# Decoder attention: VectorE shifts two units of scores with one reduce and one add, from two neighbouring PSUM banks

## The chip, the cores and the metric

The kernel runs on one core of one Trainium2 chip. The metric is device time in microseconds, from the first to the last instruction of one execution. The engines are called PE (TensorE matmul), DVE (VectorE), ACT (ScalarE), POOL (GpSimd) and SP (SyncE, which only issues DMAs here). Each engine runs its own instructions strictly in the order in which the program lists them, and semaphores tie the engines together.

## The reference, cut to what matters

The program is a two-layer transformer block on 32 sequences of 128 tokens with 128 features. It has six stages, each followed by a layer norm: attention, windowed cross attention and routed experts in the first layer, and causal attention with rotary embedding, a gated recurrence and routed experts in the second. The change touches only the causal attention, which has 16 heads of 8 features:

```
qkv = x @ w_qkv
Q, K, V = split(qkv)                    # 16 heads of 8
Q, K = apply_rope(Q), apply_rope(K)
attn = einsum('bqhd,bkhd->bhqk', Q, K) * head_dim ** -0.5
attn = where(causal, attn, -1e9)
attn = softmax(attn, axis=-1)           # exp(attn - max) / sum
out = einsum('bhqk,bkhd->bqhd', attn, V).reshape(B, S, dim) @ w_proj + b_proj
x = layernorm(x + out)
```

## The kernel before

The kernel is one program with a function for each group of stages. `phase_decode` holds the decoder attention. It works sequence by sequence (32 of them, index `b`) and cuts the 16 heads of a sequence into four *units* of four heads, so there are 128 units. One unit's scores are 128 queries by 4 x 128 keys in fp32, which fill one PSUM bank exactly. The tensor `quad` (`d_bank_scores`) is four banks next to each other, one for each unit of a sequence.

Time is cut into *ticks*, one for each unit, and every engine has one loop over the same ticks. `due(tick, offset)` says whether a step of some sequence falls on this tick; each such step falls on every fourth tick. Four ticks, in which the four units u0 to u3 of one sequence pass, are called a *frame* here. The order within an engine is thus written out by hand, and nothing reorders it.

What one frame holds on each engine, in its order, with the lines of the kernel before:

- PE: at tick 3 of a frame it writes the causal mask into banks 2 and 3 (L1644), then adds the next sequence's scores to all four banks (L1651), and signals `scores_done`. After that come, for units u2 and u3 of the frame and u0 and u1 of the next, the turning of the probabilities (`turn`, L1660) and the product with the values (`weigh`, L1672). In between stand: the turn back of an output (L1747, `mix_back`), the projections of the coming sequence into the bank `vec_bank` (L1704, `qk_done`) and of its values (L1709), two turns (L1717 and L1724), the output projection (L1729), and at tick 2 the mask for banks 0 and 1.
- DVE: for each unit the negated row maximum (L1802, `d_neg_max`) and the add that shifts the scores (L1806, into the ring `sc`, signal `shifted`). After u0 it scales a mixed output out of `vec_bank` (L1809 reciprocal and L1812 multiply, signal `mix_scaled`), after u1 it takes the rotary products from `vec_bank` (L1819, `d_halves`), and after u3 come eleven small instructions of two layer norms (L1828 to L1903).
- ACT: for each unit the exponential (L1765, waits for `shifted`), and the copy of the turned probabilities (L1783). Between them stand copies of other banks: the mixed output (L1762), the turned mix (L1772, `d_mixT`, signal `mixT_ready`), the values (L1768) and others.

`vec_bank` and `act_bank` are each shared by several steps in turn, so waits order them: PE may write the projections (L1704) only once DVE has scaled the output that lay in `vec_bank` (L1812), and may turn x4 into `act_bank` (L1724) only once ACT has taken `mixT` from it (L1772). In code:

```
if (n := due(tick, -8)) is not None:          # PE, tick 0 of a frame
    pe.wait_ge(x4T_ready, n + 1)
    if n >= 4:
        pe.wait_ge(mix_scaled, n - 3)
...
if (n := due(tick, -10)) is not None:         # PE, tick 2 of a frame
    pe.wait_ge(x4_ready, n + 1)
    if n >= 5:
        pe.wait_ge(mixT_ready, n - 4)
```

Of the kernel before, what the change touches and what calls it, by code (L numbers as in the profile page):

```python
# [14 lines left out]
P = 128  # L15
# [88 lines left out]
def bcast(ap, n):  # L104

    return ap.unsqueeze(2).to_broadcast([ap.shape[0], ap.shape[1], n])
# [1422 lines left out]
def phase_decode(nc, c, d, keep, scr, xT_all, experts1, recur):  # L1529
# [4 lines left out]
    with Phase(nc) as ctx:  # L1534
# [3 lines left out]
        def tiles(name, shape, n=2):  # L1538
            return ring(nc, ctx, "d_" + name, shape, n)

        def bank(name):
# [8 lines left out]
                                    tiles("x4_bo", [P, P], 7))  # L1550
        halves, qk, k_place, va = (tiles("halves", [P, G, P]), tiles("q_k_rotated", [P, 2, P]), tiles("k_by_place", [P, G, P]),
                                   tiles("values", [P, HEADS, VC], 4))
        nmax, sc, pr, pt = (tiles("neg_max", [P, G], 4), tiles("scores", [P, G, P], 4), tiles("probs", [P, G, P], 3),
                            tiles("probs_t", [P, G * P]))
        ot, rs, mix, mixT = tiles("mix_t", [P, G * P]), tiles("rsum", [P, HEADS]), tiles("mix", [P, P]), tiles("mixT", [P, P])
        sub5, x5 = tiles("sub5", [P, P]), tiles("x5", [P, P])
# [83 lines left out]
        @block.tensor  # L1640
        def _(pe):
            def mask(b, g):

                nc.tensor.matmul(quad[:, g, :], lhsT=c["ident_bf"][:], rhs=repeat(c["causal_bf"][:], G), start=True, stop=False)  # L1644

            def scores(b):

                pe.wait_ge(k_ready, b + 1)
                for g in range(G):
                    rows = slice(32 * g, 32 * g + 32)  # L1650
                    last = nc.tensor.matmul(quad[:, g, :], lhsT=qk[b % 2][rows, 0, :],  # L1651
                                            rhs=k_place[b % 2][rows, :, :].rearrange("p j u -> p (j u)"), start=False, stop=True)
                last.then_inc(scores_done, 1)

            def turn(u):
                pe.wait_ge(probs_ready, u + 1)
                if u:
                    pe.wait_ge(probs_t_ready, u)
                for j in range(G):
                    last = nc.tensor.transpose(turned_bank[:, j * P:(j + 1) * P], pr[u % 3][:, j, :], c["ident"][:])  # L1660
                last.then_inc(probs_turned, 1)

            def weigh(u):

                b, g = divmod(u, G)
                pe.wait_ge(probs_t_ready, u + 1)
                if g == 0:
                    pe.wait_ge(v_ready, b + 1)
                    if b:
                        pe.wait_ge(mix_copied, b)  # L1670
                for j in range(G):
                    last = nc.tensor.matmul(mix_bank[32 * j:32 * j + VC, g * P:(g + 1) * P], lhsT=va[b % 4][:, G * g + j, :],  # L1672
                                            rhs=pt[u % 2][:, j * P:(j + 1) * P], start=True, stop=True)
                last.then_inc(mixed, 1)

            pe.wait_ge(buffers_set, 2)
            for g in range(G):
                mask(0, g)
            for tick in TICKS:
                b, g = divmod(tick, G)  # L1680
                if g == G - 1 and 0 <= b + 1 < BATCH:
                    if b >= 0:
                        for bank in (2, 3):
                            pe.wait_ge(shifted, b * G + bank + 1)
                            mask(b + 1, bank)
                    scores(b + 1)
                if g == 1 and 2 <= tick < UNITS_ALL + 2:
                    weigh(tick - 2)
                if 1 <= tick <= UNITS_ALL:
                    turn(tick - 1)  # L1690
                if g != 1 and 2 <= tick < UNITS_ALL + 2:
                    weigh(tick - 2)
                if g == 2 and 0 <= b < BATCH - 1:
                    for bank in (0, 1):
                        pe.wait_ge(shifted, b * G + bank + 1)
                        mask(b + 1, bank)
                if (n := due(tick, -8)) is not None:
                    pe.wait_ge(x4T_ready, n + 1)
                    if n >= 4:
                        pe.wait_ge(mix_scaled, n - 3)  # L1700
                    elif n:
                        pe.wait_ge(halves_ready, n)
                    for k, name in enumerate(("l_wq", "l_wk", "l_wqp", "l_wkp")):
                        last = nc.tensor.matmul(vec_bank[:, k * P:(k + 1) * P], lhsT=c[name][:], rhs=x4T[n % 2][:],  # L1704
                                                start=True, stop=True)
                    last.then_inc(qk_done, 1)
                    if n >= 7:
                        pe.wait_ge(x5T_ready, n - 6)
                    nc.tensor.matmul(act_bank[:, 0:P], lhsT=x4T[n % 2][:], rhs=c["l_wv"][:], start=True, stop=True)\  # L1709
                        .then_inc(v_done, 1)  # L1710
                if (n := due(tick, 9)) is not None:
                    pe.wait_ge(mix_scaled, n + 1)
                    if n + 4 < BATCH:
                        pe.wait_ge(v_ready, n + 5)
                    else:
                        pe.wait_ge(x5T_ready, n - 2)
                    nc.tensor.transpose(act_bank[:, 0:P], mix[n % 2][:], c["ident"][:]).then_inc(mix_turned, 1)  # L1717
                if (n := due(tick, -10)) is not None:
# [3 lines that stand above are left out]
                    elif n:  # L1722
                        pe.wait_ge(v_ready, n)
                    nc.tensor.transpose(act_bank[:, 0:P], x4[n % 2][:], c["ident"][:]).then_inc(x4_transposed, 1)  # L1724
                if (n := due(tick, 10)) is not None:
                    pe.wait_ge(mixT_ready, n + 1)
                    if n + 4 < BATCH:
                        pe.wait_ge(halves_ready, n + 5)
                    nc.tensor.matmul(vec_bank[:, 0:P], lhsT=mixT[n % 2][:], rhs=c["l_wo"][:], start=True, stop=True)\  # L1729
                        .then_inc(attn_done, 1)  # L1730
                if (n := due(tick, 19)) is not None:
                    pe.wait_ge(x5_ready, n + 1)
                    if n + 7 < BATCH:
                        pe.wait_ge(x4T_ready, n + 8)
                    elif n + 2 < BATCH:
                        pe.wait_ge(mixT_ready, n + 3)
                    else:
                        pe.wait_ge(x5T_ready, n)
                    nc.tensor.transpose(act_bank[:, 0:P], x5[n % 2][:], c["ident"][:]).then_inc(x5_turned, 1)
                if (n := due(tick, 7)) is not None:  # L1740
                    pe.wait_ge(mix_copied, n + 1)
                    if n:
                        pe.wait_ge(joined5, n)
                    else:
                        pe.wait_ge(halves_ready, 4)
                    for k in range(G):
                        last = nc.tensor.transpose(vec_bank[:, k * P:(k + 1) * P], ot[n % 2][:, k * P:(k + 1) * P], c["ident"][:])  # L1747
                    last.then_inc(mix_back, 1)
                if -21 <= tick < -4:
                    stream(nc, c, turned_bank[:, 0:2 * P])  # L1750
                if tick == UNITS_ALL + 4:
                    pe.wait_ge(probs_t_ready, UNITS_ALL)
                if UNITS_ALL + 4 <= tick:
                    stream(nc, c, turned_bank[:, 0:P])

        @block.scalar
        def _(act):
            act.wait_ge(buffers_set, 2)
            for tick in TICKS:
# [1 line left out]
                    act.wait_ge(mixed, G * b + G)  # L1761
                    nc.scalar.activation(ot[b % 2][:], mix_bank[:], ACT.Copy).then_inc(mix_copied, 1)  # L1762
                if 0 <= tick < UNITS_ALL:
                    act.wait_ge(shifted, tick + 1)
                    nc.scalar.activation(pr[tick % 3][:], sc[tick % 4][:], ACT.Exp).then_inc(probs_ready, 1)  # L1765
                if (b := due(tick, -7)) is not None:
                    act.wait_ge(v_done, b + 1)
                    nc.scalar.activation(va[b % 4][:, :, 0:DH], act_bank[:, 0:P].rearrange("p (h d) -> p h d", d=DH), ACT.Copy)\  # L1768
# [18 lines left out]
        def _(dve):  # L1787
# [7 lines left out]
            chain = Chain(dve, links, 0, 0)  # L1795

            for tick in TICKS:
                if 0 <= tick < UNITS_ALL:
                    b, g = divmod(tick, G)
                    dve.wait_ge(scores_done, b + 1)  # L1800
                    bank = quad[:, g, :].rearrange("p (j u) -> p j u", j=G)
                    nc.vector.tensor_reduce(nmax[tick % 4][:], bank, AX.X, ALU.max, negate=True).then_inc(max_ready, 1)  # L1802
                    dve.wait_ge(max_ready, tick + 1)
                    if tick >= 4:
                        dve.wait_ge(probs_ready, tick - 3)
                    nc.vector.tensor_tensor(sc[tick % 4][:], bank, bcast(nmax[tick % 4][:], P), ALU.add).then_inc(shifted, 1)  # L1806
                if (b := due(tick, 8)) is not None:
                    dve.wait_ge(mix_back, b + 1)
                    nc.vector.reciprocal(rs[b % 2][:], vec_bank[:].rearrange("p (h c) -> p h c", c=VC)[:, :, DH])\  # L1809
# [742 lines left out]
```

## Time and profile before

| | us |
|---|---|
| three runs | 1351.29, 1352.99, 1353.49 (median 1352.99) |
| the profiled execution | 1351.8 |
| its span in the trace | 1350.0 |
| busy in the span: PE / DVE / ACT / POOL | 1180.8 / 1043.2 / 855.9 / 555.8 |
| decoder attention, first to last start of L1802 | 810.9 to 1093.2 |
| of that, L1806 x128 / L1802 x128 busy | 88.5 / 87.4 |

The span is from the first instruction to the last in the trace. Busy is the sum of the instructions' own durations on an engine; a group that is pipelined can look busy while it does not run at its peak. The decoder attention takes some 285 of the 1350 us.

### The profile page before, as it was taken

Reading aid. Unit: us, or ns where it says so; the run is one execution under the profiler, and the core shown is the slowest. Engines: PE = TensorE matmul, PEld = TensorE weight load, DVE = VectorE, ACT = ScalarE, POOL = GpSimd, SP = SyncE. Lnnn points to the kernel's source line nnn. Section 1 sums busy time; section 2 is a strip of 40 time slices with the busy share of each in tenths; the row PEclk is TensorE's granted clock in tenths of the full one; section 3 lists DMA queues with packets and bytes.
Section 4 is the critical chain, followed back from the end, with each engine's and each line's share of the span. In section 5 each row is a group of like instructions: output and inputs, shape, how many; then the busy total and the mean of one; then the engine's idle time right before and its main releaser. Section 6 shows DMA issues by size and latency. Waiting matters only on the chain. (4 is left out here: it accounts for less than half of the span.)

```text
span 1350.0 us, 31833 instructions
## 1 busy us (share of the span) xinstructions
PE 1180.8 (87%) x10209; PEld 817.6 (61%) x10209; DVE 1043.2 (77%) x3188; ACT 855.9 (63%) x2442; POOL 555.8 (41%) x831
## 2 busy tenths in 40 slices
PE   3789999999999999887399978999999979999796
PEld 2556665666666666654266655555555557767796
DVE  4578889888888888876688858999999965665465
ACT  2678888888788878854166625666666654453464
POOL 1233334434353535351400046555555312556387
PEclk9999999999999999997599988999999989999898
DMA  6200000000010100000222222103000000000673
GB/s 225 95 15 15 17 15 23 24 19 29 17 33 15 31 11 25 10 20 11 65 81 82 83 57 90 38 24 97 25 21 19 2 3 1 17 17 25 180 211 93
DMA packets 71490, 63.54 MB, mean 47 GB/s; under 512 B 10510, under 2 KB 61586, under 8 KB 70688
## 3 DMA queue, kind: packets, MB, share of 16 engines
q1 hardware_dynamic: 62768, 45.27, 11.4%
q0 software_dynamic: 6400, 12.63, 3.0%
q10 hardware_dynamic: 2160, 3.60, 0.8%
q8 instruction: 87, 1.43, 0.4%
q14 instruction: 75, 0.61, 0.1%
HBM read 45.10 MB, written 16.88 MB: 46 GB/s over the span
## 5 line engine op out<-in xcount | busy, mean ns | idle before, releaser
L783 PE MATMUL e_bank_turned<-c_matrices,e_probs 128*128 128x128 f32 x1024 | 164.6, 285 | 19.0 <-ACT e_probs_t L1008 9.2
L709 POOL TENSOR_TENSOR e_rstd<-e_var_eps,c_minus_half 128x1 f32<-128x1 f32 x128 | 71.2, 570 | 234.6 <-DVE e_var_eps L1049 233.7
L1008 ACT ACTIVATE e_probs_t<-e_bank_turned 128x512 f32<-128x512 f32 x256 | 154.8, 605 | 14.5 <-PE e_bank_turned L783 12.9
L1136 DVE TENSOR_REDUCE e_neg_max<-e_bank_scores 128x4 f32<-128x512 f32 x160 | 109.7, 685 | 49.2 <-PE e_bank_scores L827 48.4
L783 PEld LDWEIGHTS e_bank_turned<-c_matrices,e_probs 128*128 128x128 f32 x1024 | 115.8, 144 | 43.8 <-issue 22.6
L793 PE MATMUL e_bank_mix<-e_probs_t,e_values 128*32 128x128 f32 x2048 | 111.6, 291 | 16.0 <-ACT e_probs_t L1008 15.8
L971 ACT ACTIVATE e_probs<-e_scores,e_neg_max 128x128 f32<-128x128 f32 x384 | 123.4, 411 | 1.1 <-DVE e_neg_max L1172 1.1
L1783 ACT ACTIVATE d_probs_t<-d_bank_turned 128x512 f32<-128x512 f32 x128 | 77.2, 603 | 66.1 <-PE d_bank_turned L1660 66.1
L966 ACT ACTIVATE e_probs<-e_scores 128x512 f32<-128x512 f32 x128 | 81.7, 638 | 43.0 <-DVE e_scores L1169 41.3
L712 POOL TENSOR_TENSOR e_k_by_place<-e_q_k_k,c_matrices 128x512 f32<-128x512 f32 x64 | 66.7, 1042 | 100.4 <-DVE e_q_k_k L1180 100.4
L1765 ACT ACTIVATE d_probs<-d_scores 128x512 f32<-128x512 f32 x128 | 81.0, 633 | 41.0 <-DVE d_scores L1806 39.3
L1660 PE MATMUL d_bank_turned<-c_matrices,d_probs 128*128 128x128 f32 x512 | 82.3, 284 | 24.7 <-ACT d_probs_t L1783 23.6
L1660 PEld LDWEIGHTS d_bank_turned<-c_matrices,d_probs 128*128 128x128 f32 x512 | 55.6, 142 | 61.4 <-issue 56.6
L1806 DVE TENSOR_TENSOR d_scores<-d_bank_scores,d_neg_max 128x512 f32<-128x512 f32 x128 | 88.5, 692 | 4.4
L1802 DVE TENSOR_REDUCE d_neg_max<-d_bank_scores 128x4 f32<-128x512 f32 x128 | 87.4, 683 | 5.7 <-PE d_bank_scores L1651 5.5
L1169 DVE TENSOR_TENSOR e_scores<-e_bank_scores,e_neg_max 128x512 f32<-128x512 f32 x128 | 88.3, 690 | 3.4
L1601 POOL DMA_INDIRECT d_first<-scratch_expert_out,keep_out_rows x32 | 32.2, 1005 | 137.8 <-POOLq L85 132.1
L793 PEld LDWEIGHTS e_bank_mix<-e_probs_t,e_values 128*32 128x32 f32 x2048 | 40.8, 109 | 63.0 <-issue 33.8
L1342 PE MATMUL m_wide<-up,m_rowsT 128*128 x144 | 75.8, 609 | 0.4 <-ACT m_rowsT L1407 0.2
L720 POOL DMA_INDIRECT scratch_sorted<-e_x,e_row_u x64 | 64.3, 1005 | 26.5 <-issue 15.8
L2120 ACT ACTIVATE n_states<-n_bank_drive 128x32 f32<-128x32 f32 x128 | 25.3, 198 | 65.1 <-PE n_bank_drive L2046 63.0
L1138 DVE TENSOR_TENSOR e_scores<-e_bank_scores,c_bias 128x512 f32<-128x512 f32 x96 | 65.7, 684 | 0.0
(324 smaller groups left out, 3232.7 us busy)
## 6 DMA issues: line engine op xcount, KB each, us to landing
streamed<-in_s_up SPq DMA_DIRECT2D x36, 258.0 KB, 2.9
sorted_rows<-scratch_sorted SPq DMA_DIRECT2D x72, 64.0 KB, 1.8
scratch_expert_out<-m_y SPq DMA_DIRECT2D x72, 64.0 KB
sorted_rows<-scratch_sorted SPq DMA_DIRECT2D x40, 65.0 KB, 2.3
e_xT_ctxT<-in_xT SPq DMA_DIRECT2D x32, 64.0 KB
e_xT_ctxT<-in_ctxT SPq DMA_DIRECT2D x32, 64.0 KB
e_x_in<-in_x SPq DMA_DIRECT2D x32, 64.0 KB, 1.8
up<-in_m_wgv SPq DMA_DIRECT2D x1, 2048.0 KB
```

Of the source, the lines that this page charges most:

```text
L783: last = nc.tensor.transpose(turned_bank[:, j * P:(j + 1) * P], pr[k % 3][:, j, :], c["ident"][:])
L793: last = nc.tensor.matmul(mix_bank[32 * j:32 * j + VC, g * P:(g + 1) * P], lhsT=va[att][n % 3][:, G * g + j, :], rhs=pt[k % 2][:, j * P:(j ...
L966: nc.scalar.activation(pr[k % 3][:], sc[k % 4][:], ACT.Exp).then_inc(probs_ready, 1)
L971: last = nc.scalar.activation(pr[k % 3][:, j, :], src[:, j, :], ACT.Exp, bias=nmax[k % 4][:, j:j + 1], scale=1.0)
L1008: nc.scalar.activation(pt[k % 2][:], turned_bank[:], ACT.Copy).then_inc(probs_t_ready, 1)
L1136: nc.vector.tensor_reduce(nmax[k % 4][:], bank, AX.X, ALU.max, negate=True).then_inc(max_ready, 1)
L1169: nc.vector.tensor_tensor(sc[k % 4][:], bank, bcast(nmax[k % 4][:], P), ALU.add).then_inc(bank_read, 1)
L1660: last = nc.tensor.transpose(turned_bank[:, j * P:(j + 1) * P], pr[u % 3][:, j, :], c["ident"][:])
L1765: nc.scalar.activation(pr[tick % 3][:], sc[tick % 4][:], ACT.Exp).then_inc(probs_ready, 1)
L1783: nc.scalar.activation(pt[(tick - 1) % 2][:], turned_bank[:], ACT.Copy).then_inc(probs_t_ready, 1)
L1802: nc.vector.tensor_reduce(nmax[tick % 4][:], bank, AX.X, ALU.max, negate=True).then_inc(max_ready, 1)
L1806: nc.vector.tensor_tensor(sc[tick % 4][:], bank, bcast(nmax[tick % 4][:], P), ALU.add).then_inc(shifted, 1)
```

## The change

DVE now works at ticks 0 and 2 of a frame only, each time on two banks: one reduce over 128 x 8 x 128 scores and one add of the same size. The ring `sc` has two buffers of two units in place of four of one, and `shifted` counts pairs. ACT's exponentials stay one for each unit, and each waits for its pair. PE waits for a pair before it writes the masks of two banks. Nothing else is touched; lines below the edit move by one.

```diff
-        nmax, sc, pr, pt = (tiles("neg_max", [P, G], 4), tiles("scores", [P, G, P], 4), tiles("probs", [P, G, P], 3),
+        nmax, sc, pr, pt = (tiles("neg_max", [P, 2 * G], 4), tiles("scores", [P, 2 * G, P]), tiles("probs", [P, G, P], 3),
...
                     if b >= 0:
+                        pe.wait_ge(shifted, 2 * b + 2)
                         for bank in (2, 3):
-                            pe.wait_ge(shifted, b * G + bank + 1)
                             mask(b + 1, bank)
...
                 if g == 2 and 0 <= b < BATCH - 1:
+                    pe.wait_ge(shifted, 2 * b + 1)
                     for bank in (0, 1):
-                        pe.wait_ge(shifted, b * G + bank + 1)
                         mask(b + 1, bank)
...
                 if 0 <= tick < UNITS_ALL:
-                    act.wait_ge(shifted, tick + 1)
-                    nc.scalar.activation(pr[tick % 3][:], sc[tick % 4][:], ACT.Exp).then_inc(probs_ready, 1)
+                    pair, half = divmod(tick, 2)
+                    act.wait_ge(shifted, pair + 1)
+                    nc.scalar.activation(pr[tick % 3][:], sc[pair % 2][:, half * G:(half + 1) * G, :], ACT.Exp).then_inc(probs_ready, 1)
...
-                if 0 <= tick < UNITS_ALL:
-                    b, g = divmod(tick, G)
+                if 0 <= tick < UNITS_ALL and tick % 2 == 0:
+                    (b, g), pair = divmod(tick, G), tick // 2
                     dve.wait_ge(scores_done, b + 1)
-                    bank = quad[:, g, :].rearrange("p (j u) -> p j u", j=G)
-                    nc.vector.tensor_reduce(nmax[tick % 4][:], bank, AX.X, ALU.max, negate=True).then_inc(max_ready, 1)
-                    dve.wait_ge(max_ready, tick + 1)
-                    if tick >= 4:
-                        dve.wait_ge(probs_ready, tick - 3)
-                    nc.vector.tensor_tensor(sc[tick % 4][:], bank, bcast(nmax[tick % 4][:], P), ALU.add).then_inc(shifted, 1)
+                    banks_of_pair = quad[:, g:g + 2, :].rearrange("p g (j u) -> p (g j) u", j=G)
+                    nc.vector.tensor_reduce(nmax[pair % 4][:], banks_of_pair, AX.X, ALU.max, negate=True).then_inc(max_ready, 1)
+                    dve.wait_ge(max_ready, pair + 1)
+                    if pair >= 2:
+                        dve.wait_ge(probs_ready, tick - 2)
+                    nc.vector.tensor_tensor(sc[pair % 2][:], banks_of_pair, bcast(nmax[pair % 4][:], P), ALU.add).then_inc(shifted, 1)
```

The first place is DVE's order in one frame. Before, from the first reduce of a frame to the first instruction of its layer norms (the names are tiles, written `out<-in`):

```order
L1802 TENSOR_REDUCE d_neg_max<-d_bank_scores 128x4
L1806 TENSOR_TENSOR d_scores<-d_bank_scores,d_neg_max 128x512
L1809 RECIPROCAL d_rsum<-d_bank_vec 128x16
L1812 TENSOR_TENSOR d_mix<-d_bank_vec,d_rsum 128x128
L1802 TENSOR_REDUCE d_neg_max<-d_bank_scores 128x4
L1806 TENSOR_TENSOR d_scores<-d_bank_scores,d_neg_max 128x512
L1819 TENSOR_TENSOR d_halves<-d_bank_vec,c_rope 128x512
L1802 TENSOR_REDUCE d_neg_max<-d_bank_scores 128x4
L1806 TENSOR_TENSOR d_scores<-d_bank_scores,d_neg_max 128x512
L1802 TENSOR_REDUCE d_neg_max<-d_bank_scores 128x4
L1806 TENSOR_TENSOR d_scores<-d_bank_scores,d_neg_max 128x512
```

And the same stretch of DVE's row with the change:

```order
L1803 TENSOR_REDUCE d_neg_max<-d_bank_scores 128x8
L1807 TENSOR_TENSOR d_scores<-d_bank_scores,d_neg_max 128x1024
L1810 RECIPROCAL d_rsum<-d_bank_vec 128x16
L1813 TENSOR_TENSOR d_mix<-d_bank_vec,d_rsum 128x128
L1820 TENSOR_TENSOR d_halves<-d_bank_vec,c_rope 128x512
L1803 TENSOR_REDUCE d_neg_max<-d_bank_scores 128x8
L1807 TENSOR_TENSOR d_scores<-d_bank_scores,d_neg_max 128x1024
```

The work of u1 has moved ahead of the scaling (L1809, L1812), and nothing stands between the scaling and the rotary products (L1819) any more.

The second place is ACT's order from tick 2 of a frame to tick 3, the same before and with the change but for the numbers of the lines; here with the change, where both exponentials wait for the pair u2, u3:

```order
L1762 ACTIVATE d_mix_t<-d_bank_mix 128x512
L1766 ACTIVATE d_probs<-d_scores 128x512
L1773 ACTIVATE d_mixT<-d_bank_act 128x128
L1784 ACTIVATE d_probs_t<-d_bank_turned 128x512
L1766 ACTIVATE d_probs<-d_scores 128x512
```

The copy of `mixT` and the copy of the turned probabilities of u1 stand behind the exponential of u2, as before.

## Rows read from the trace of the kernel before

**Rows 1.** Busy us (x count) of PE, PEld, DVE, ACT, POOL; granted clock; DMA share, GB/s.

```profile
950.00:1000.00 50.00, 45.63 (x437) 28.08 (x435) 47.33 (x124) 32.66 (x74) 28.67 (x38) 1.00 0.08 24
```

**Rows 2.** Timeline of DVE: the first reduce of frames 2 and 30.

```profile
829.38 0.69 DVE L1802 TENSOR_REDUCE d_neg_max<-d_bank_scores 128x4 f32<-128x512 f32 x1 [0.26 <-PE d_bank_scores L1651]
...
1080.35 0.69 DVE L1802 TENSOR_REDUCE d_neg_max<-d_bank_scores 128x4 f32<-128x512 f32 x1 [0.51 <-PE d_bank_scores L1651]
```

**Rows 3.** Timeline of one frame: start, us, engine, instruction, [idle before <-releaser].

```profile
953.76 0.59 PE L1644 MATMUL d_bank_scores<-c_causal_bf,c_ident_bf 128*128 128x512 bf16 x2
...
955.50 0.69 DVE L1802 TENSOR_REDUCE d_neg_max<-d_bank_scores 128x4 f32<-128x512 f32 x1 [0.19 <-PE d_bank_scores L1651]
956.22 0.69 DVE L1806 TENSOR_TENSOR d_scores<-d_bank_scores,d_neg_max 128x512 f32<-128x512 f32 x1
...
957.11 0.26 DVE L1809 RECIPROCAL d_rsum<-d_bank_vec 128x16 f32<-128x16 f32 x1 [0.19 <-PE d_bank_vec L1747]
957.40 0.29 DVE L1812 TENSOR_TENSOR d_mix<-d_bank_vec,d_rsum 128x128 f32<-128x128 f32 x1
...
957.61 0.68 DVE L1802 TENSOR_REDUCE d_neg_max<-d_bank_scores 128x4 f32<-128x512 f32 x1
957.83 1.13 PE L1704 MATMUL d_bank_vec<-d_x4T,c_matrices 128*128 128x128 f32 x8
958.32 0.69 DVE L1806 TENSOR_TENSOR d_scores<-d_bank_scores,d_neg_max 128x512 f32<-128x512 f32 x1
959.05 0.63 ACT L1765 ACTIVATE d_probs<-d_scores 128x512 f32<-128x512 f32 x1 [0.77 <-DVE d_scores L1806]
959.17 0.69 DVE L1819 TENSOR_TENSOR d_halves<-d_bank_vec,c_rope 128x512 f32<-128x512 f32 x1 [0.16 <-PE d_bank_vec L1704]
...
959.78 0.68 DVE L1802 TENSOR_REDUCE d_neg_max<-d_bank_scores 128x4 f32<-128x512 f32 x1
...
960.91 0.63 PE L1660 MATMUL d_bank_turned<-c_matrices,d_probs 128*128 128x128 f32 x4 [0.62 <-ACT d_probs_t L1783]
961.23 0.63 ACT L1765 ACTIVATE d_probs<-d_scores 128x512 f32<-128x512 f32 x1
...
962.27 0.27 PE L1724 MATMUL d_bank_act<-c_matrices,d_x 128*128 128x128 f32 x1
...
962.60 0.59 PE L1644 MATMUL d_bank_scores<-c_causal_bf,c_ident_bf 128*128 128x512 bf16 x2
```

**Rows 4.** Timeline at the decoder's end: PE waits for the scaled mix.

```profile
1100.98 0.29 DVE L1812 TENSOR_TENSOR d_mix<-d_bank_vec,d_rsum 128x128 f32<-128x128 f32 x1
...
1101.33 0.48 PE L1717 MATMUL d_bank_act<-c_matrices,d_mix 128*128 128x128 f32 x1 [0.38 <-DVE d_mix L1812]
```

**Rows 5.** Timeline of frame 1: DVE waits for the projections.

```profile
823.07 1.16 PE L1704 MATMUL d_bank_vec<-d_x4T,c_matrices 128*128 128x128 f32 x8
...
824.27 0.69 DVE L1819 TENSOR_TENSOR d_halves<-d_bank_vec,c_rope 128x512 f32<-128x512 f32 x1 [0.68 <-PE d_bank_vec L1704]
```

**Rows 6.** Timeline of frame 14: u2's exponential, the copy behind it, and PE.

```profile
943.34 0.63 ACT L1765 ACTIVATE d_probs<-d_scores 128x512 f32<-128x512 f32 x1 [0.63 <-DVE d_scores L1806]
943.87 0.26 ACT L1772 ACTIVATE d_mixT<-d_bank_act 128x128 f32<-128x128 f32 x1
...
944.28 0.30 PE L1724 MATMUL d_bank_act<-c_matrices,d_x 128*128 128x128 f32 x1 [0.40 <-ACT d_mixT L1772]
```

**Rows 7.** The same columns in frame 0 and behind the last frame.

```profile
817.50:820.00 2.50, 2.50 (x12) 0.80 (x10) 1.59 (x5) 0.28 (x1) 2.40 (x5) 0.50 0.58 131
...
1097.50:1100.00 2.50, 1.28 (x12) 0.66 (x13) 0.38 (x2) 1.27 (x4) 0.00 (x0) 1.00 0.00 0
1100.00:1102.50 2.50, 2.10 (x10) 1.62 (x11) 1.44 (x6) 1.85 (x4) 0.55 (x1) 0.63 0.00 0
```

**Rows 8.** Timeline of frame 0: masks to the next reduce.

```profile
817.70 1.06 PE L1644 MATMUL d_bank_scores<-c_causal_bf,c_ident_bf 128*128 128x512 bf16 x2
...
820.85 0.69 DVE L1802 TENSOR_REDUCE d_neg_max<-d_bank_scores 128x4 f32<-128x512 f32 x1 [1.69 <-PE d_bank_scores L1651]
```

## The prediction

> **What bounds the kernel now.** I read the busy time by stretch first. In 950 to 1000 us, steady decoder work, DVE is busy 47.33 of 50 us and PE 45.63 at the full clock [rows 1]. Two engines that are both over 90% busy invite the conclusion that work taken off DVE shortens the stage. Busy time cannot decide that, since two in-order engines that wait for each other in turn can both look full. So I read the timeline next, frame by frame. Frames 2 to 29, 28 of them, take 1080.35 - 829.38 = 250.97 us, or 8.96 us each [rows 2].
>
> One frame [rows 3] is followed from the mask of banks 2 and 3 at 953.76 to the same mask at 962.60, 8.84 us later. The scores let DVE's first reduce start 1.74 us after the mask; DVE had waited 0.19 for it. The reciprocal at 957.11 had waited 0.19 for PE's turn back, not for DVE's own work, so u0's reduce and add had that much slack. After the scaling at 957.40, PE writes the projections into the same bank at 957.83, and DVE takes the rotary products at 959.17, having waited 0.16 us. Between the scaling and the rotary products DVE did the whole of u1 (957.61 and 958.32). That work covered the way to PE and back. Further on, PE turns u1's probabilities at 960.91 after a wait of 0.62 for ACT, and reaches the turn of x4 at 962.27 and the next mask at 962.60. ACT began u2's exponential at 961.23 without an idle gap.
>
> The frame is therefore a ring of short hops through PE, DVE and ACT, with slack of only tenths. I price the change on that ring.
>
> **What the change does to DVE's own time.** An instruction over 512 columns lets the next one start 0.61 us later (959.17 to 959.78), one over 128 columns 0.21 (957.40 to 957.61): 0.40 us for 384 columns, so 512 more columns cost 0.53 [rows 3]. Reduce to add, where the add must wait for the reduce's result, takes 0.72 (955.50 to 956.22) and should become 0.72 + 0.53 = 1.25. Add to the next instruction should become 0.61 + 0.53 = 1.14. A pair takes 2.39 where two units took 2 x (0.72 + 0.61) = 2.66: 0.27 less, and 0.27 x 64 = 17 us over all pairs. No row shows a DVE instruction that reads two banks. The dearest case is no saving at all, 1.44 and 1.22. For the other end I allow 0.1 us off a whole frame, from the spread of equal hops in the rows. I take the extrapolation, since a doubled instruction is nearest to the row of 512 columns plus its slope.
>
> The page "Advanced Engine Details and Errata" of the Trainium skill, section "The Read-Write Bubble", advises large tiles of 512 or 1024 elements, and one instruction over several PSUM banks, to pay a gap between instructions less often. The slope above bears the advice out as far as DVE's own time goes; by that alone the sum would be the third rival below.
>
> **Ring, first half: the scaling comes late.** The scaling now stands behind the work of both units. From the mask: 1.74 to the reduce, 1.25 to the add, 1.14 to the reciprocal, 0.29 to the multiply (957.11 to 957.40) [rows 3]. From the multiply to PE I have 0.35 where PE waited (1100.98 to 1101.33) [rows 4] and 0.43 in the frame, where PE may have had work of its own; I take 0.40. That makes 4.82 us from the mask to the projections, against 957.83 - 953.76 = 4.07. PE's earlier work, which took the 4.07, no longer sets it. Queued behind the waiting projections are the values' projection, the product for u3 and the turn of the next u0; all come 0.75 later.
>
> **Ring, second half: the cover is gone.** DVE's next instruction is the one that waits for those projections. They took 1.20 us to reach DVE where it really waited, 0.68 us of it (823.07 to 824.27) [rows 5], and 1.34 in the frame of [rows 3]; I take 1.20. Then 0.61 to the reduce of u2 and u3, and 1.25 to their add. ACT's exponential began 0.73 after an add's start (958.32 to 959.05, a real wait) [rows 3] and now begins 0.73 + 0.53 = 1.26 after it. So u2's exponential starts 1.20 + 0.61 + 1.25 + 1.26 = 4.32 us after the projections; before it was 961.23 - 957.83 = 3.40.
>
> What is queued behind that exponential decides. The copy of `mixT` follows 0.53 later (943.34 to 943.87), and PE may turn x4 0.41 after that, a row in which PE did wait 0.40 for it [rows 6]; 0.33 more brings the next mask (962.27 to 962.60) [rows 3]. In the frame before, 961.23 + 0.53 + 0.41 = 962.17 was 0.10 ahead of the turn at 962.27: hidden, but barely. Now the sum is 4.32 + 0.53 + 0.41 + 0.33 = 5.59 us from the projections to the next mask, against 962.60 - 957.83 = 4.77.
>
> **The rest of the edit costs nothing.** The wait for masks 2 and 3 is over long before: the add of u2 and u3 ends about 1.25 us after its start, at the time ACT's exponential begins, and the mask stands 1.27 behind that (0.53 + 0.41 + 0.33). The masks of banks 0 and 1 wait for a pair that is done before PE's projections start. The smaller ring of buffers waits for exponentials of the pair two before, a frame earlier. DVE's layer norms now begin 1.26 + 1.27 - 1.14 = 1.39 us before the mask; in [rows 3] the first reduce waited for the scores though DVE came from the same norms, so the first hop stays at 1.74. POOL's preparation of the keys starts with the rotary products, and the mask ahead of the scores now comes 5.59 - 1.20 = 4.39 us after these, where it was 962.60 - 959.17 = 3.43.
>
> **The sum.** 4.82 + 5.59 = 10.41 us a frame in place of 8.96: 1.45 x 28 = 40.6 us. At both ends the first exponential of a pair comes 1.25 + 1.26 - (0.72 + 0.73) = 1.06 later. I put 2 us for the two ends. The profiled execution took 1351.8 us (span 1350.0), so 1351.8 + 42.6 = 1394 us. The median of the runs, 1352.99, is 1.2 above that execution, less than any case here differs by.
>
> If a pair saves nothing, each frame adds 2 x 0.19 for the reduces, 0.08 before the reciprocal and 0.20 before the exponential, 0.66 x 28 = 18 us: 1412. If the hops are 0.1 shorter, it is 1391.
>
> **Rivals.**
>
> *Only the first half counts.* If the copy of `mixT` is not what PE waits for, the second half stays as it is and the frame grows by 0.75: 21 us and 2 at the ends, 1375. For it: in the frame of [rows 3] PE did not wait at that turn. Against it: the slack was 0.10, and the exponential comes 0.92 later.
>
> *PE's clock falls.* PE would idle some 2.2 us of each 10.4: 0.75 ahead of the projections, 0.62 ahead of u1's turn as now, 0.82 ahead of the turn of x4. Behind the last frame a stretch with PE busy 1.28 of 2.5 us was followed by one at a mean granted clock of 0.63, a fall to 1.2 GHz from 2.4 [rows 7]. In the new frame the last two of these gaps, 1.44 us, fall within some 3 us, not far from that row's 1.22 idle in 2.5. At 1.2 GHz (0.50 in the stretch of frame 0 [rows 7]) the hop from mask to reduce took 3.15 us (817.70 to 820.85) [rows 8] and not 1.74. A third of the frames at that price add 9 x 1.41 = 13: 1407. All of them would give 1434.
>
> *DVE is the bound, and the time falls.* Then the 17 us saved are gained: 1335. For it: 47.33 of 50 us [rows 1]. It is also what the advice on large tiles quoted above from the Trainium skill comes to. It holds only if the hops from scaling to rotary products, 0.40 + 1.20 less the 0.21 that DVE spends there anyway, 1.39 us, came to less than the 0.54 that a frame saves. Against it: [rows 5] shows DVE waiting when nothing covers that way.
>
> *The change doesn't do what it says.* If PE's own work sets the frame whatever DVE does, nothing moves: 1352. Against it: the reciprocal now comes 1.25 + 1.14 = 2.39 us after the first reduce, where it was 957.11 - 955.50 = 1.61 [rows 3], and 0.19 us of slack do not cover 0.78.
>
> **How the numbers follow.** Chances: the forecast 0.62, the falling clock 0.17, only the first half 0.10, DVE as the bound 0.06, no change 0.05. A measurement of this kernel tells about 0.2% from nothing, some 3 us. So faster 0.06, same 0.05, slower 0.89. The range takes in the first rival at its low end and, at the high end, the pair without savings and a clock that falls in more than a third of the frames: 1372 to 1418.
>
> **What would show it.** Right: frames of about 10.4 us; L1803 and L1807 near 1.2 us each; L1820 waiting about a microsecond for PE's L1704 in each frame; ACT's L1766 waiting for DVE before u2, and PE waiting for ACT's L1773 before it turns x4; DVE's share down to some 75%. Wrong: L1820 without a wait, frames under 9 us, or a granted clock below 1.00 in the middle of the decoder, which would put the time above the forecast.

## The result, and the profile after

The changed kernel is slower: a median of 1400.57 us in 4 runs (1395.99 to 1403.88) against 1353.24 for the kernel before on the same chip (1351.29 to 1353.72), a ratio of 1.035 with a 95% interval of 1.0326 to 1.0374. Its profiled execution took 1403.88 us, its span is 1402.0.

Busy time by stretch, kernel after, columns as in [rows 1]:

```profile
950.00:1000.00 50.00, 40.42 (x379) 24.51 (x378) 37.94 (x89) 27.79 (x63) 24.34 (x33) 1.00 0.28 71
```

DVE is down from 47.33 us of 50 to 37.94 and PE from 45.63 to 40.42, at the full granted clock. Every engine has more free time, which fits engines that wait for each other; the timeline below shows the waits. The DMA share is higher because the weights of the next stage begin to load at 951.16 us here and at 927.21 before; the frames are as long outside that burst. Next the timeline of DVE, kernel after, first reduces of frames 2 and 30, as in [rows 2]:

```profile
837.69 1.22 DVE L1803 TENSOR_REDUCE d_neg_max<-d_bank_scores 128x8 f32<-128x1024 f32 x1 [0.69 <-PE d_bank_scores L1651]
...
1131.33 1.23 DVE L1803 TENSOR_REDUCE d_neg_max<-d_bank_scores 128x8 f32<-128x1024 f32 x1 [0.51 <-PE d_bank_scores L1651]
```

The 28 frames take 293.64 us, 10.49 each, where they took 8.96. One of them, timeline of PE, DVE and ACT in the kernel after, as in [rows 3]:

```profile
961.88 0.59 PE L1644 MATMUL d_bank_scores<-c_causal_bf,c_ident_bf 128*128 128x512 bf16 x2
...
963.62 1.23 DVE L1803 TENSOR_REDUCE d_neg_max<-d_bank_scores 128x8 f32<-128x1024 f32 x1 [0.44 <-PE d_bank_scores L1651]
...
964.87 1.23 DVE L1807 TENSOR_TENSOR d_scores<-d_bank_scores,d_neg_max 128x1024 f32<-128x1024 f32 x1
...
966.01 0.25 DVE L1810 RECIPROCAL d_rsum<-d_bank_vec 128x16 f32<-128x16 f32 x1
...
966.30 0.29 DVE L1813 TENSOR_TENSOR d_mix<-d_bank_vec,d_rsum 128x128 f32<-128x128 f32 x1
...
966.74 1.13 PE L1704 MATMUL d_bank_vec<-d_x4T,c_matrices 128*128 128x128 f32 x8 [0.76 <-DVE d_mix L1813]
...
967.90 0.69 DVE L1820 TENSOR_TENSOR d_halves<-d_bank_vec,c_rope 128x512 f32<-128x512 f32 x1 [1.31 <-PE d_bank_vec L1704]
...
968.51 1.21 DVE L1803 TENSOR_REDUCE d_neg_max<-d_bank_scores 128x8 f32<-128x1024 f32 x1
...
969.76 1.23 DVE L1807 TENSOR_TENSOR d_scores<-d_bank_scores,d_neg_max 128x1024 f32<-128x1024 f32 x1
...
971.02 0.63 ACT L1766 ACTIVATE d_probs<-d_scores 128x512 f32<-128x512 f32 x1 [0.86 <-DVE d_scores L1807]
971.55 0.26 ACT L1773 ACTIVATE d_mixT<-d_bank_act 128x128 f32<-128x128 f32 x1
...
971.96 0.30 PE L1724 MATMUL d_bank_act<-c_matrices,d_x 128*128 128x128 f32 x1 [0.63 <-ACT d_mixT L1773]
972.09 0.45 PE L1729 MATMUL d_bank_vec<-c_matrices,d_mixT 128*128 128x128 f32 x2
...
972.38 0.59 PE L1644 MATMUL d_bank_scores<-c_causal_bf,c_ident_bf 128*128 128x512 bf16 x2
```

Read it as a relay. PE stands 0.76 us until DVE has scaled the mix behind the adds of both units; DVE then stands 1.31 us, its dearest idle spot in the decoder, until the projections are there; PE stands 0.63 until ACT has copied `mixT` behind u2's exponential. From the mask of banks 2 and 3 to the projections it is 4.86 us, from the projections to the next such mask 5.64. Over the whole run, groups of DVE's instructions in the kernel after (count | busy us, mean ns | idle ahead):

```profile
L1807 DVE TENSOR_TENSOR d_scores<-d_bank_scores,d_neg_max 128x1024 f32<-128x1024 f32 x64 | 78.4, 1224 | 2.2
L1803 DVE TENSOR_REDUCE d_neg_max<-d_bank_scores 128x8 f32<-128x1024 f32 x64 | 78.0, 1219 | 16.8 <-PE d_bank_scores L1651 16.8
L1820 DVE TENSOR_TENSOR d_halves<-d_bank_vec,c_rope 128x512 f32<-128x512 f32 x32 | 22.1, 690 | 37.7 <-PE d_bank_vec L1704 37.7
```

DVE did become cheaper: 78.4 + 78.0 us of add and reduce, where the two groups took 88.5 and 87.4 before. What it saved went into waiting, 37.7 us of it in one place.

The two spans differ by 52.0 us: 42.7 in the 28 frames, 0.7 ahead of frame 2, 1.0 behind the start of frame 30, and 7.6 before the decoder's first reduce (818.44 against 810.9), in stages that the edit does not touch. That last part is not the change's: in the ten kernels below, which are all alike ahead of the decoder, this reduce starts between 809.88 and 818.74 us.

### The profile page after: what moved, and what is told of

It is laid out like the page before. It is cut to its first block and busy times, and to the rows that moved or that the text cites. A ratio compares the mean times of both kernels' runs of the same rounds, so it can differ in the third digit from the quotient of the medians.

```text
span 1402.0 us, 31643 instructions
## 1 busy us (share of the span) xinstructions
PE 1192.8 (85%) x10209; PEld 819.5 (58%) x10209; DVE 1029.0 (73%) x3060; ACT 854.8 (61%) x2442; POOL 553.7 (39%) x831
## 5 line engine op out<-in xcount | busy, mean ns | idle before, releaser
L1803 DVE TENSOR_REDUCE d_neg_max<-d_bank_scores 128x8 f32<-128x1024 f32 x64 | 78.0, 1219 | 16.8 <-PE d_bank_scores L1651 16.8
L1807 DVE TENSOR_TENSOR d_scores<-d_bank_scores,d_neg_max 128x1024 f32<-128x1024 f32 x64 | 78.4, 1224 | 2.2
L1172 DVE TENSOR_REDUCE e_neg_max<-e_scores 128x4 f32<-128x512 f32 x96 | 64.8, 675 | 0.3
```

Source lines behind the costliest of these rows:

```text
L1803: nc.vector.tensor_reduce(nmax[pair % 4][:], banks_of_pair, AX.X, ALU.max, negate=True).then_inc(max_ready, 1)
L1807: nc.vector.tensor_tensor(sc[pair % 2][:], banks_of_pair, bcast(nmax[pair % 4][:], P), ALU.add).then_inc(shifted, 1)
```

## The experiments

All kernels are in one table; "frame" is the mean of the 28 frames of [rows 2], the two halves of the ring are means over frames 6 to 25, and "rest" is the span from the decoder's first reduce to the end. Ratios are to the kernel before in the same batch (its medians 1352.57, 1350.56 and 1350.35).

| kernel | median us | ratio (95%) | frame | mask to proj. | proj. to mask | rest |
|---|---|---|---|---|---|---|
| before | 1353.24 | | 8.96 | 4.07 | 4.95 | 539.1 |
| after | 1400.57 | 1.035 (1.0326-1.0374) | 10.49 | 4.85 | 5.64 | 583.6 |
| early pair only | 1376.70 | 1.018 (1.0161-1.02) | 9.67 | 4.91 | 4.76 | 559.7 |
| late pair only | 1395.09 | 1.0306 (1.0285-1.0327) | 10.35 | 4.16 | 6.33 | 580.0 |
| both, copy first | 1375.41 | 1.0171 (1.0153-1.0189) | 9.62 | 4.85 | 4.77 | 558.7 |
| both, scaling between | 1396.37 | 1.0327 (1.03-1.0353) | 10.16 | 4.10 | 6.16 | 579.6 |
| late pair, gather moved | 1376.68 | 1.0206 (1.0177-1.0234) | 9.78 | 4.09 | 5.72 | 561.4 |
| late pair, copy first | 1352.18 | 1.0009 (0.9991-1.0026) | 8.87 | 4.07 | 4.82 | 536.2 |
| both, all moved | 1354.17 | 1.0025 (1.001-1.0041) | 8.88 | 4.07 | 4.83 | 538.8 |
| before, copy first | 1350.62 | 1.0 (0.9984-1.0016) | 8.90 | 4.07 | 4.86 | 535.5 |
| before, gather moved | 1354.80 | 1.0019 (0.9999-1.0039) | 8.91 | 4.17 | 4.77 | 535.4 |
| late, copy first, gather moved | 1353.67 | 1.002 (0.9999-1.004) | 8.89 | 4.15 | 4.76 | 537.0 |

The theory is the ring: a pair costs what stands behind it in DVE's and ACT's queues. One rival is that the pair itself, the wait for two banks, sets the price; another is PE's clock.

**Each pair alone.** From the kernel before; the early pair reads `g != 1` and `g == 0` in place of `g != 3` and `g == 2`.

```diff
-                if 0 <= tick < UNITS_ALL:
-                    b, g = divmod(tick, G)
+                b, g = divmod(tick, G)
+                if 0 <= tick < UNITS_ALL and g != 3:
+                    units, pair, low = 2 if g == 2 else 1, tick // 2, g % 2 * G
```

Early pair (u0 and u1):

> Only u0 and u1 are taken as a pair; u2 and u3 stay single, as before. Theory: mask to projections stays at 4.85 us as in the changed kernel; u2's exponential then starts 1.17 + 0.61 + 0.72 + 0.73 = 3.23 us after the projections, before ACT is free for it at 3.40, so the second half is that of before, 4.77 to 4.98; frames of 9.62 to 9.83, 1372 to 1378. Rival A (all of the loss comes from the late scaling): frames stay at 10.5, 1396 to 1400. If only the late exponential counted: 8.96, 1353.

1376.70 us, as expected. The first half took 4.91 us, 0.84 more than before; the second took 4.76, which is what the shortest frames before took (their mean is 4.95). A frame costs 0.71 us more, though u2's exponential is not late: the late scaling has that price by itself.

Late pair (u2 and u3):

> Only u2 and u3 are taken as a pair; u0 and u1 stay single, with the scaling between them, as before. Theory (two hops of the ring, each with its own price): mask to projections goes back to 4.07 us, projections to the next mask stays at the 5.64 of the changed kernel, since u2's exponential still waits for the pair; frames of 9.71 us, 0.75 x 28 = 21 us over before: about 1374. Rival A (all of the loss comes from the late scaling): frames of 8.96, 1353. Rival B (a DVE instruction that reads two banks is itself what slows its neighbours): the hops around the pair lengthen and not the waits, about 1375 as well, but with DVE's add over 1.3 us or PE's and ACT's instructions on those banks longer.

1395.09 us: a miss by 21. The first half was as before, but the hop from the projections to the rotary products took 1.74 to 1.84 us in 20 frames instead of 1.17. (In two frames the granted clock fell as well; they took 11.98 and 11.87 us.) Timeline of POOL, PE and DVE in this kernel, one such frame and the one frame between them that was spared:

```profile
957.90 1.13 PE L1704 MATMUL d_bank_vec<-d_x4T,c_matrices 128*128 128x128 f32 x8
958.19 0.96 POOL L1601 DMA_INDIRECT d_second<-scratch_expert_out,keep_out_rows  x1 [0.30 <-issue]
...
959.70 0.69 DVE L1823 TENSOR_TENSOR d_halves<-d_bank_vec,c_rope 128x512 f32<-128x512 f32 x1 [0.63 <-PE d_bank_vec L1704]
...
968.80 0.95 POOL L1601 DMA_INDIRECT d_second<-scratch_expert_out,keep_out_rows  x1 [0.30 <-issue]
...
970.30 1.13 PE L1704 MATMUL d_bank_vec<-d_x4T,c_matrices 128*128 128x128 f32 x8 [0.38 <-issue]
...
971.46 0.69 DVE L1823 TENSOR_TENSOR d_halves<-d_bank_vec,c_rope 128x512 f32<-128x512 f32 x1
```

Where POOL's second gather of a coming sequence's rows starts 0.29 us behind the projections, the rotary products start 1.80 behind them; where it starts 1.50 ahead, 1.16. PE's own time is 1.13 in both. The spared frame is one of the two in which the clock fell (0.59 in 965 to 968): its projections came 5.91 us behind the mask, not 4.07, and the gather had not waited for them. So a third thing seemed to be in this ring, and the next kernel moves only that.

**Late pair, gather moved.** In each frame the two gathers now stand right behind POOL's preparation of the keys, ahead of its three small layer-norm steps and no longer behind them. The expectations call this later; for a given sequence it is one tick earlier.

```diff
-                if (b := due(tick, -25)) is not None:
+                if (b := 0 if tick == FIRST else due(tick, -26)) is not None:
                     gather(b)
```

> The kernel with only the late pair (u2 and u3), and POOL's gather of the next frame issued after its placing of the mask's row, one step later in the tick than before. Theory that the frames of the late-pair kernel were long because DVE's rotary products wait while POOL issues the second gather 0.3 us behind the projections: the hop from the projections to the halves goes back from 1.74 to 1.84 us to 1.17, frames take about 9.68 us, and the run about 1,374 to 1,378 us, some 20 us less than the late pair alone. Rival, that the late pair itself makes that hop long (the gather only happens to lie there): frames stay at 10.4 us and the run at 1,392 to 1,396. In between: the gather meets another DVE instruction of the ring instead (the layer norms ahead of the reduce), and the loss shows there as a longer hop from the projections' first row to the mask.

1376.68 us, 18 less. Timeline of POOL, PE and DVE in this kernel:

```profile
954.83 0.96 POOL L1601 DMA_INDIRECT d_second<-scratch_expert_out,keep_out_rows  x1 [0.30 <-issue]
...
959.34 1.13 PE L1704 MATMUL d_bank_vec<-d_x4T,c_matrices 128*128 128x128 f32 x8
...
960.51 0.69 DVE L1823 TENSOR_TENSOR d_halves<-d_bank_vec,c_rope 128x512 f32<-128x512 f32 x1
```

The hop was 1.17 (1.16 to 1.18) in all of the 28 frames. They took 9.78 us, 0.1 more than expected. The late pair with the gather out of the way costs 0.82 us a frame, of which 0.77 lie in the second half, as the theory has it.

**Both pairs, copy of `mixT` first.** From the changed kernel, on ACT:

```diff
+                if (b := due(tick, 10)) is not None:
+                    act.wait_ge(mix_turned, b + 1)
+                    nc.scalar.activation(mixT[b % 2][:], act_bank[:, 0:P], ACT.Copy).then_inc(mixT_ready, 1)
                 if 0 <= tick < UNITS_ALL:
...
-                if (b := due(tick, 10)) is not None:
-                    act.wait_ge(mix_turned, b + 1)
-                    nc.scalar.activation(mixT[b % 2][:], act_bank[:, 0:P], ACT.Copy).then_inc(mixT_ready, 1)
```

> Both pairs, as in the changed kernel; ACT copies mixT ahead of u2's exponential instead of behind it, so that nothing of PE's stands behind that wait. Theory: mask to projections 4.85, projections to the next mask back to 4.77 to 4.98: frames of 9.62 to 9.83, about 1375, some 20 us less than the changed kernel. Rival A (all of the loss comes from the late scaling): no gain, frames stay at 10.5. Rival B (the two-bank instructions themselves): no gain either.

1375.41 us. Timeline of ACT and PE in this kernel:

```profile
950.89 0.28 ACT L1765 ACTIVATE d_mixT<-d_bank_act 128x128 f32<-128x128 f32 x1
...
951.86 0.63 ACT L1769 ACTIVATE d_probs<-d_scores 128x512 f32<-128x512 f32 x1 [0.69 <-DVE d_scores L1807]
952.02 0.27 PE L1724 MATMUL d_bank_act<-c_matrices,d_x 128*128 128x128 f32 x1
952.13 0.39 PE L1729 MATMUL d_bank_vec<-c_matrices,d_mixT 128*128 128x128 f32 x2
...
952.35 0.59 PE L1644 MATMUL d_bank_scores<-c_causal_bf,c_ident_bf 128*128 128x512 bf16 x2
```

The copy is done before u2's exponential begins, PE no longer waits at L1724, and the second half is back at 4.77. One copy of 128 columns, placed behind an exponential that it does not need, was 0.87 us a frame.

**Both pairs, scaling between reduce and add.** From the changed kernel; `scale` is the reciprocal and the multiply.

```diff
                     nc.vector.tensor_reduce(nmax[pair % 4][:], banks_of_pair, AX.X, ALU.max, negate=True).then_inc(max_ready, 1)
+                    if (n := due(tick, 8)) is not None:
+                        scale(n)
                     dve.wait_ge(max_ready, pair + 1)
```

> Both pairs; DVE scales the mixed output between the reduce and the add of the first pair instead of behind the add, so that the add covers the way to PE and back. Theory: mask to projections back to 4.07. But u0's exponential now comes later, 3.84 + 1.26 = 5.10 us after the mask, and ACT's copy of the turned u3 of the frame before stands behind it (5.8), for which PE's product waits: that would carry u0's turn to about 6.9 and the next mask to 10.0 to 10.3. So the frame hardly gains, 10.0 to 10.3: 1384 to 1391. Without this last wait the frame would be 9.72, 1376. Rival A (all of the loss comes from the late scaling): 8.96, 1353.

1396.37 us, only 4 less than the changed kernel and 5 above the expected range. The first half fell to 4.07 in ordinary frames, as expected, but the next step in line became the wait. Timeline of ACT and PE in this kernel:

```profile
899.59 0.37 ACT L1781 ACTIVATE xT_all<-d_bank_act 128x128 f32<-128x128 f32 x1
...
900.01 0.49 PE L1709 MATMUL d_bank_act<-c_matrices,d_x4T 128*128 128x128 f32 x2 [0.85 <-ACT xT_all L1781]
```

PE's value projection waits 0.85 us for another copy that ACT keeps behind an exponential, that of u0, which the pair made late. The expectation had named the copy of the turned u3, which stands next behind the same exponential. Ordinary frames take 9.96 us, just below the 10.0 to 10.3 expected. In four of the 28 the granted clock falls as well; busy time by stretch, columns as in [rows 1]:

```profile
878.00:881.00 3.00, 1.79 (x17) 1.26 (x18) 2.97 (x5) 2.58 (x8) 1.77 (x2) 0.96 0.08 22
881.00:884.00 3.00, 3.00 (x18) 1.73 (x18) 0.85 (x4) 2.17 (x6) 0.00 (x0) 0.50 0.33 113
```

0.50 is 1.2 GHz; PE had been busy 1.79 of 3 us ahead of the fall. Such frames take 11.5 us, which lifts the mean to 10.16 and the run by some 6 us.

**Both pairs, all of these moved.** The scaling between, and ACT's copies of `mixT`, of `xT_all` and of the turned u3 ahead of the exponentials.

> Both pairs, as in the changed kernel, with all the steps that the ring was found to wait for moved ahead: the scaling between the first pair's reduce and subtraction, ACT's copy of mixT ahead of the exponential of u2, its copies of the value input and of the turned u3 ahead of the exponential of u0. Theory that pairing costs only by what stands behind the pair in the queues: frames of 8.84 to 9.1 us, 1,349 to 1,356 us, about as the kernel before. If the wait for both banks itself (PE's second bank, not the queue) sets the price: frames of 9.6 us or more and over 1,371 us. If clock falls come, as with the scaling moved alone, single frames show 1 us or more on top and a mean of 9.2 to 9.3.

1354.17 us, frames of 8.88. The pairs are all still there, and the loss is gone but for 0.25%. Busy time by stretch:

```profile
950.00:1000.00 50.00, 47.13 (x447) 29.15 (x446) 44.88 (x98) 33.32 (x74) 29.86 (x39) 1.00 0.09 23
```

DVE is 2.45 us lighter than in [rows 1] and PE 1.50 fuller. From the decoder's first reduce to the end the profiled execution takes 538.8 us, before 539.1. The 28 frames gained 2.2 us, and the ends gave most of it back: the granted clock fell at the very end (0.70 in 1086 to 1089), and the last frame took 10.24 us, before 8.13. One profile of each does not settle where the 0.25% lies. What holds the frame at 8.9 is probably PE, busy 94% here; no run took work off PE, so that is argued only.

**Late pair, copy first.**

> The late pair alone, with ACT's copy of mixT put ahead of the exponential of u2, so that the projections no longer wait for that exponential. Without a meeting with POOL's gather the first half of the ring takes 4.07 us and the second, now free of the copy behind the exponential, about 4.8 to 5.0: frames of 8.84 to 9.05 us, 1,350 to 1,356 us, no different from the kernel before. If the gather still meets the rotary products (0.6 us more in most frames): 9.4 to 9.6 us and 1,366 to 1,371 us. If pairing as such costs more than the order of ACT's copy, frames stay above 10 us and the run above 1,385.

1352.18 us, no difference from before. Once the copy stands ahead of it, the pair of u2 and u3 costs nothing that shows (at most 0.26% by the interval).

**Control: the kernel before, copy first.**

> Control: the kernel before, with only ACT's copy of mixT put ahead of the exponential of u2. In the kernel before the exponential of u2 ends 1.7 us or so behind its bank and the copy stands behind it, but there the add of u2 and the exponential come after the mask's subtraction of another tick. If the copy waits for it there too, frames shrink from 8.96 to 8.84 us and the run to 1,349 to 1,350 us; if not, 1,352 to 1,353, no difference. Either way the move alone gives no 25 us, so that what it gives back in the changed kernel is the price of the pair and not a gain that was there to be had anyway.

1350.62 us, ratio 1.0, with frames of 8.90 us, between the 8.84 and the 8.96 of the two cases. What the move returns in the changed kernel is the pair's price, not a gain that lay there anyway.

**The gather in the kernel before, and with the late pair.**

> The kernel before, with only POOL's gathers issued after the placing of the mask's row (as in the late pair with the later gather). Theory that a gather that starts some 0.5 to 0.84 us behind the projections holds DVE's rotary products: the hop from the projections to the halves goes from a mean of 1.33 us to 1.17 in every frame, ordinary frames from 8.97 to 8.83, and the run 3 to 5 us down, to about 1,346 to 1,348. If the gather in its new place holds another DVE instruction of the ring (as the layer norm and the late subtraction were held by 0.05 to 0.1 us in the late pair with the later gather), the gain is 1 us or none. If the gather has nothing to do with it, the hop keeps its 1.33 and the run its 1,351 to 1,353.

> The late pair with ACT's copy of mixT first and the gathers later. By the same theory the hop from the projections to the halves goes from a mean of 1.36 us to 1.17. The second half of the ring is then 0.2 us shorter, unless the first half and the other rings of the frame stand at 8.83 us already, which is the shortest frame of the run without the later gather: frames of 8.83 us throughout, 1,349 to 1,351 us against 1,352 for the one with the gather in its old place. A pair that beat the kernel before by 0.2% or more (below 1,348 us) would show that the pair itself is of use once its wait is covered; 1,349 or more, that the frame is then set by something that the pair does not touch.

Neither is faster: 1354.80 and 1353.67, where 1346 to 1348 and 1349 to 1351 were expected. The hop to the rotary products did fall to 1.17 in every frame of both (means of 1.33 and 1.36 without the move), but part of it was lost ahead of the first reduce. Timeline of POOL, PE and DVE in the kernel before with the gather moved:

```profile
951.30 0.60 PE L1644 MATMUL d_bank_scores<-c_causal_bf,c_ident_bf 128*128 128x512 bf16 x2
...
951.79 0.96 POOL L1601 DMA_INDIRECT d_second<-scratch_expert_out,keep_out_rows  x1 [0.30 <-issue]
951.83 1.14 PE L1651 MATMUL d_bank_scores<-d_k_by_place,d_q_k_rotated 32*128 32x512 f32 x8
...
953.36 0.69 DVE L1802 TENSOR_REDUCE d_neg_max<-d_bank_scores 128x4 f32<-128x512 f32 x1 [0.29 <-PE d_bank_scores L1651]
```

From mask to reduce it is now 2.06 us instead of 1.74, and 2.02 to 2.09 in 21 of the 22 steady frames in which a gather lies beside the wait for the scores; it is 1.73 in those without one. Most of that is hidden, since the reciprocal had waited for PE's turn back anyway [rows 3]: the first half grows by 0.1 on the mean. Two frames, at which a drain on POOL stands right ahead of the gather, lost 0.5 and 0.9 us more. In the profiled executions the frames take 8.91 us, for 8.96 before, and with the late pair 8.89, for 8.87; why the first of the two runs is not shorter is open. No version tried here beats the kernel before by what can be told.

## Why the prediction was right

**The forecast case happened, by its own mechanism.** 1394 was forecast, 1400.57 measured, inside the range. Of the profiled execution's 52 us, 44.4 are the decoder's; 42.6 were forecast.

- *DVE's own time.* Reduce to add took 1.25 (forecast 1.25), add to reciprocal 1.14 (1.14). The pair takes 2.39 us, 0.27 less than two units. The frame still grew by 1.52 us. By the Trainium skill, "Advanced Engine Details and Errata", section "The Read-Write Bubble", large tiles and one instruction over several banks are the way to pay the gap between instructions less often. The trace agrees as far as DVE's own time goes (2.39 us for 2.66); the third rival, which took the saving for time gained, failed.
- *The scaling comes late.* From mask to projections it took 4.86 us, forecast 4.82. The early pair alone shows this half by itself.
- *The cover is gone.* Projections to rotary products took 1.16 (1.20), DVE waiting 1.31 us.
- *What is queued behind u2's exponential decides.* Add to exponential 1.26 (1.26), to the copy 0.53 (0.53), to L1724 0.41 (0.41). Taking the copy out of this queue took 0.87 us a frame with it.
- *The mis-sized term.* L1724 to the mask was 0.42, not 0.33, in every steady frame. The forecast took 0.33 from [rows 3], where PE came to L1724 without a wait. Behind a wait for the copy, L1724 and L1729 take 0.30 and 0.45 us, as above; without, 0.27 and 0.39, as in the kernel with the copy first. [rows 6] had shown the 0.30: in five of 26 frames of the kernel before, L1724 already started 0.40 or 0.41 us behind the start of the copy, and in each of these the mask came 0.42 later. With +0.04 from multiply to projections and -0.04 to the rotary products this makes 10.49 in place of 10.41, 2 us over all.
- *The ends* came to 1.7 us, forecast 2. The rest of the median's excess, some 5 us, is not the mechanism's; it fits the spread of the stages ahead of the decoder (8.9 us over the profiled runs); why these vary is open.

**The rivals.** Only the first half: the early pair alone gives that rival's time, 1376.70 against 1375, and the changed kernel is 24 us above it. The clock did not fall in the changed kernel's steady frames, though PE idles about 2 us in each. DVE was not the bound: it got lighter, and the time rose. Two banks in one instruction are no cost in themselves: with the copies and the scaling moved, both pairs run at 8.88 us a frame.

## What to carry to other kernels

Before merging instructions on a busy in-order engine, list what stood between them and whose round trip that covered, and what is queued behind the first reader of the merged result. If the ring is tight, move those short steps ahead of the merged instruction in the same edit; here three copies and a scaling were worth some 44 of the 47 us lost, and the pairs then gained nothing. A busy share of 95% tells nothing of gain when a second engine stands at 91% and the two wait for each other.

## What was not expected of the hardware

An indirect gather that POOL issues can hold a DVE instruction that waits for PE. In the late pair the rotary products started about 1.51 us behind the start of the gather, 0.6 later than PE's results allowed; in the kernel before the same hop had a mean of 1.33 us where the shortest is 1.16; with the gather moved, the scores' reduce came late instead, 1.57 behind the gather's start. The held instruction is no slower in itself (0.69 us).

The held starts keep time with the gather and not with PE. Where the hop was longer than 1.22 us, the rotary products started 0.68 to 0.81 us behind the gather's start (12 frames of the kernel before, 22 of the kernel with all moved) or 1.46 to 1.63 behind it (two frames of the kernel before, 20 of the late pair, two with the scaling between); the held reduce started 1.53 to 1.60 behind it in 21 frames. In the frame of [rows 3], in the kernel before, the gather was this one, and the rotary products started 0.79 behind it, at 959.17:

```profile
958.38 0.96 POOL L1601 DMA_INDIRECT d_second<-scratch_expert_out,keep_out_rows  x1 [0.30 <-issue]
```

The Trainium skill, "SBUF — State Buffer", section "Who interferes with whom", says that a DVE instruction with at most one SBUF input, outside the two-port modes, does not contend with GpSimd. The rotary products read one SBUF operand and PSUM, and their unchanged 0.69 us agree; the section does not speak of late starts. Whether the signal from PE or DVE's start is held is open. Nor does the gather's place alone decide it: with the scaling between, a gather 0.28 to 0.30 us behind the projections left the hop at 1.17, and one 0.04 to 0.06 behind gave 1.58 to 1.63.

The clock fell in a few frames of the kernel with the scaling between (0.50 in 881 to 884), in two of the late pair alone, and in none of the steady frames of the changed kernel, though PE is busier with the scaling between (42.41 of 50 us in 950 to 1000) than in the changed kernel (40.42). Which gaps matter was not separated.
